# Two-batch windowed attention plus mixture of experts on one core: parts of 16, 12 and 4 tiles, another place for the routing arithmetic, and result rows written by ScalarE

## The chip, the cores and the metric

The kernel runs on 1 core of one Trainium2 chip. The metric is the device time of one execution in microseconds. Five engines work side by side and meet only through semaphores: TensorE (PE; its weight loads are PEld), VectorE (DVE), ScalarE (ACT), GpSimd (POOL) and SyncE (SP, which here only issues DMAs). An engine works through its own list of instructions strictly in the order in which they are written, so that whatever stands behind a wait waits too.

## The reference, cut to what matters

```python
# x: (2, 2048, 128) = 4096 tokens = 32 tiles of 128
x = layernorm(x + attention(x))      # 16 query heads, 4 key/value heads of 8, window of 128 on each side
x = layernorm(x + moe(x))

# moe:
probs   = softmax(x @ router)                      # 8 experts
w, idx  = top_k(probs, 2);  w = softmax(w)
fuse    = silu(x @ gating[e]) * (x @ up[e])        # 128 -> 256, of the two chosen experts
out     = sum over the two of w * (fuse @ down[e]) # 256 -> 128
```

All is float32.

## The kernel before, in words

**Attention steps.** Steps `s` run from -2 to 31, one per tile of 128 tokens, and every engine has its function `step(s)`. A step computes, interleaved, five score items "A" of tile s+2 (only their maxima are wanted) and five items "B" of tile s (exponentials, then the products with the values). Items go in turn through three PSUM banks `pX`. DVE takes the maxima of the A items (`largest_score(a, 0)` to `(a, 4)`, L1311 and L1315), ACT the exponentials of the B items (L1051). PE can't write an item before the one three places earlier is read: item B2 waits for the maximum of A1, item B3 for that of A2. Between these DVE finishes tile s-1: reciprocal `rden` (L1359), `attT` (L1362), residual sum (L1371), statistics (L1378); POOL normalises four tiles at a time (`norm`, L621 to L631).

**Routing.** Eight tiles at a time form a routing group: 21 small DVE operations (`rt_op`, with two exponentials on ACT) give the two experts and their weights. PE counts ranks (`ranks`, L824 and L828), ACT copies them out (L1079), 8 DVE operations (`slot_op`) make the rows' places. `RT_AT`, `RANK_AT` and `SLOT_AT` say in which step each stands. 19 DVE operations per part (`table_op`) make the tables by which the units find their rows and experts. POOL writes each tile's rows, sorted by expert, to DRAM (`sort_rows`, two indirect DMAs per tile, L648).

**Parts and units.** `PARTS` cuts the 32 tiles into parts that are sorted separately: 16, 8 and 8 tiles. A part of n tiles has at most 2n+8 blocks of 128 rows; two blocks are a unit. That makes 20, 12 and 12, together 44 units, numbered k = 0 to 43. In iteration k, PE turns the rows of unit k+1 (`turn_rows`, L940), does gate and up projections of unit k (`gate_up`, L957 to L959), turns the hidden rows of k-1 (L968) and does the down projection of k-2 (L977). ACT rounds rows (L1101), does Silu (L1108), copies turned hidden rows (L1114) and results (`rows_made`, L1120). DVE makes the rest of the rounding (`rest_rows`, L1396) and the product (`hidden`, L1402). SP loads a unit's rows (`rows_in`, L533) and writes its results (L538); before unit 20, the first of part 1, it waits for all sorted rows of that part and for its table.

**The steps left over.** What is left of the steps (32 to 42, among them the whole routing group of the last eight tiles) stands in front of the units' own work in iterations 0, 1 and 3 to 11 (`MOE_STEPS`), on each engine.

**The way back.** POOL gathers both result rows of each tile, two indirect DMAs per tile in the order of the tiles (`rows_back`, L660); before the first tile of a part it waits until every result of that part has been written (`rows_done`). DVE adds them (`combine`, L1414) and normalises, from iteration `COMBINE_AT[t]` on; ACT applies the factors (L1125), SP writes the output (L544).

## Time and profile before

| What | Value |
|---|---|
| Time, median of 3 runs | 593.84 us (588.29 to 595.39) |
| Profiled execution: time, and its span | 593.14 us, 591.3 us |
| PE, PEld | 492.1 us (83%), 301.5 us (51%) |
| DVE | 359.9 us (61%) |
| ACT | 297.9 us (50%) |
| POOL | 241.4 us (41%) |
| Granted TensorE clock, mean | 0.896 |

The span is what the profile sees between the first and the last instruction; 1.84 us of the execution's time lie around it. The shares are averages over very different stretches: attention steps up to about 393 us, then units up to about 558 us, then the last gathers and sums. So the stretches have to be read one by one.

### The profile page before, as it was taken

How to read it: one execution, taken by the hardware profiler on the slowest of the kernel's cores; microseconds unless marked ns; L12 is line 12 of the kernel's file. 1: busy time of each engine (PE TensorE's matmuls, PEld its weight loads, DVE VectorE, ACT ScalarE, POOL GpSimd, SP SyncE). 2: the span in 40 equal slices, each digit the busy share in tenths (PEclk: the TensorE clock that was granted, in tenths of full speed). 3: DMA queues.
4: the chain of work that ended last, by engine and by line, in shares of the span. 5: the costliest groups of instructions: out<-in, count | busy, mean ns of one | idle time of the engine just before them, and what ended most of it. 6: DMA issues, size and time to landing. Idle time of an engine off the chain costs nothing.

```text
span 591.3 us, 12074 instructions
## 1 busy us (share of the span) xinstructions
PE 492.1 (83%) x3864; PEld 301.5 (51%) x3864; DVE 359.9 (61%) x817; ACT 297.9 (50%) x515; POOL 241.4 (41%) x329
## 2 busy tenths in 40 slices
PE   4499899899998999899898987966988999998600
PEld 3263454354453555344453533435877888886500
DVE  0366675576675887667756566553364635767674
ACT  2125554465566656456644544534565555554532
POOL 2131062462533225325435264305714517777072
PEclk9999898798999998899977877788889999999855
DMA  6452324305216352231350012020433535553252
GB/s 159 62 81 56 73 41 105 73 11 135 38 34 147 73 108 56 56 65 54 55 84 18 20 41 86 11 63 25 127 97 96 149 110 135 137 136 96 62 137 58
DMA packets 83948, 46.93 MB, mean 79 GB/s; under 512 B 40496, under 2 KB 79408, under 8 KB 83120
## 3 DMA queue, kind: packets, MB, share of 16 engines
q1 hardware_dynamic: 77184, 36.81, 27.2%
q0 software_dynamic: 4096, 8.40, 5.2%
q10 hardware_dynamic: 2608, 0.95, 0.8%
q8 instruction: 34, 0.56, 0.4%
q14 instruction: 26, 0.21, 0.1%
HBM read 26.47 MB, written 19.40 MB: 78 GB/s over the span
## 4 chain that ended last, share of the span: by engine, by line
PE 61%; DVE 15%; issue 8%; DMA 6%; ACT 3%; SPq 3%; POOL 2%; ACTq 0%; POOLq 0%; DVEq 0%
PE pV L788 13%; DVE mp L1311 6%; PE pX L977 6%; PE pX L713 5%; PE pX L957 4%; PE pX L752 4%; PE pX L959 4%; PE pX L958 3%; DMA xt<-xT 3%; PE pV L968 3%; DVE rden L1359 3%; PE pM L807 3%; PE pX L743 2%; PE pX L764 2%; SPq L427 2%
## 5 line engine op out<-in xcount | busy, mean ns | idle before, releaser
L1311 DVE TENSOR_REDUCE mp<-pX 128x4 f32<-128x1024 f32 (+4 forms) x128 | 150.2, 1186 | 96.6 <-PE pX L717 80.1
L1051 ACT ACTIVATE probs<-pX 128x1024 f32<-128x1024 f32 x152 | 152.8, 1023 | 108.7 <-PE pX L743 94.4
L788 PE MATMUL pV<-probs,vx 128*32 128x512 f32 (+1 forms) x736 | 94.4, 613 | 0.0
L660 POOL DMA_INDIRECT probs<-ys,source x64 | 64.1, 1002 | 48.1 <-issue 31.4
L648 POOL DMA_INDIRECT xs<-xr,slot x64 | 63.0, 984 | 49.5 <-DVE ends L1231 31.4
L752 PE MATMUL pX<-q,kx 50*128 50x512 f32 x248 | 64.5, 518 | 10.1 <-DVE mp L1311 9.4
L713 PE MATMUL pX<-kx,q 48*128 48x512 f32 (+4 forms) x256 | 62.1, 485 | 9.6 <-DMA q<-q_scr 9.6
L1402 DVE TENSOR_TENSOR probs<-probs,pX 128x512 f32<-128x512 f32 x44 | 30.2, 686 | 52.8 <-ACT probs L1108 52.7
L1108 ACT ACTIVATE probs<-pX 128x512 f32<-128x512 f32 x44 | 26.3, 598 | 53.6 <-PE pX L959 53.6
L713 PEld LDWEIGHTS pX<-kx,q 48*128 48x128 f32 x256 | 26.5, 205 | 50.9 <-issue 39.5
L977 PE MATMUL pX<-we,probs 128*128 x352 | 48.4, 282 | 0.7 <-ACT vx L1120 0.7
L957 PE MATMUL pX<-we,qh 128*128 x88 | 40.7, 462 | 8.0 <-issue 4.6
L977 PEld LDWEIGHTS pX<-we,probs 128*128 128x128 f32 x352 | 44.9, 200 | 1.0 <-issue 1.0
L752 PEld LDWEIGHTS pX<-q,kx 50*128 50x128 f32 x248 | 26.4, 210 | 25.0 <-DVE mp L1311 14.8
L959 PE MATMUL pX<-we,ql 128*128 x88 | 36.8, 419 | 0.0
L958 PE MATMUL pX<-we,qh 128*128 x88 | 36.3, 412 | 0.0
L588 POOL CAST kh<-ks 128x512 fp32r<-128x512 f32 x7 | 4.3, 609 | 76.1 <-ACT ks L1028 76.1
L743 PE MATMUL pX<-mask 64*128 64x256 bf16 (+1 forms) x184 | 33.8, 364 | 0.0
L1359 DVE RECIPROCAL rden<-pV 128x128 f32<-128x128 f32 x32 | 30.3, 948 | 5.6 <-PE pV L801 5.6
L601 POOL CAST qh<-qs 128x512 fp32r<-128x512 f32 x7 | 4.3, 609 | 71.4 <-ACT qs L1031 71.4
L788 PEld LDWEIGHTS pV<-probs,vx 128*32 128x32 f32 x736 | 18.3, 116 | 28.6 <-issue 23.2
L968 PE MATMUL pV<-cst,probs 128*128 128x128 f32 x176 | 28.3, 286 | 0.7 <-DVE probs L1402 0.6
(151 smaller groups left out, 827.5 us busy)
## 6 DMA issues: line engine op xcount, KB each, us to landing
q<-q_scr SPq DMA_DIRECT2D x46, 128.0 KB, 4.4
xt<-xs SPq DMA_DIRECT2D x88, 64.0 KB
ys<-vx SPq DMA_DIRECT2D x44, 128.0 KB, 1.9
...
q<-stage SPq DMA_DIRECT2D x128, 2.0 KB
...
```

What stands on the lines that cost most here:

```text
L648: pool.indirect_dma_start(xs[ph][:, :], bass.IndirectOffsetOnAxis(ap=slot[:, t, k:k + 1], axis=0), tile(t), None, bounds_check=ROWS - 1, o ...
L660: pool.indirect_dma_start(yin[:, t % YIN, k, :], None, ys[ph][:, :], bass.IndirectOffsetOnAxis(ap=source[:, t, k:k + 1], axis=0), bounds_c ...
L713: mm = pe.matmul(bank[:, pr, 0:64 * (k1 - k0)], q_cols(t, KA, pr, i, i + 1), k_cols(KA, pr, k0, k1), start=True, stop=True, skip_group_che ...
L752: mm = pe.matmul(bank[:, pr, :], k_cols(KB, pr, k0, k0 + 2), q_cols(t, KB, pr, 0, 4), start=True, stop=True, skip_group_check=True)
L788: mm = pe.matmul(pV[row:row + 32, cols], vx[:, chunk, pr, :], src[:, pr, cols], start=n == 0, stop=True, skip_group_check=True)
L957: pe.matmul(to, xh[:, k % 2, rows], hi, start=True, stop=False, skip_group_check=True)
L958: pe.matmul(to, xh[:, k % 2, rows], lo, start=False, stop=False, skip_group_check=True)
L959: mm = pe.matmul(to, xl[:, k % 2, rows], hi, start=False, stop=True, skip_group_check=True)
L977: mm = pe.matmul(pX[2][:, 1, h * D:(h + 1) * D], hidT[:, k % 2, at:at + P], we[:].bitcast(F32)[:, bass.ds(expert[k, h] + 4 * F + f * D, D) ...
L1051: act.activation(dst, src[:], ACT.Exp).then_inc(exp_done, 1)
L1311: dve.tensor_reduce(mp[:, t % 2, 0, :, i, :], src[:, :, 0:2 * n].rearrange("p r (c v k) -> p r v c k", v=NV, k=32), AX.XY, ALU.max).then_i ...
L1359: dve.reciprocal(rden[:], pV[:, P:2 * P]).then_inc(den_done, 1)
```

## The change

1. `PARTS` becomes 16, 12 and 4 tiles (20, 16 and 8 units, again 44).
2. The routing group of the last eight tiles is still computed as one, but ranked as two groups of 4 tiles (`RANKED`), each with its own ranks, copy and 8 slot operations.
3. In the attention steps DVE's slot, table and first routing operations of a step stand behind the maximum of A0, and the maximum of A1 behind them; before, they stood behind that of A1. Routing groups 0 and 1 are done in three steps and ranked a step earlier. Table 0 moves from steps 28 to 31 into 27, 30 and 31.
4. From iteration 1 on, DVE does its left-over step behind `hidden(k)`, not in front of `rest_rows(k+1)`; ACT does the two exponentials of the last routing group behind `rows_made`. That group is spread over five steps.
5. PE does `gate_up(0)` within step 32, ahead of ranks and output projection.
6. The results' DMAs are issued by ACT, right behind the copy, with a wait for it; SP has none of them.
7. Times at which parts 1 and 2 are sorted, their tables are made and zero rows are written follow the new parts.

The excerpt leaves out what only passes the two rank groups through (`rk` in two buffers, `ranks`, `slot_op`).

```diff
@@ -43,7 +43,7 @@
-PARTS = [(0, 16), (16, 24), (24, 32)]
+PARTS = [(0, 16), (16, 28), (28, 32)]
 NPH = len(PARTS)
 CAP = SEQ + P
 NJ = SEQ // P
@@ -75,9 +75,13 @@
     return next(ph for ph, (a, b) in enumerate(PARTS) if a <= t < b)
+
+RANKED = [(0, 8), (8, 16), (16, 24), (24, 28), (28, 32)]
+
+
 def groups(ph):
-    return PARTS[ph][0] // RT_TILES, PARTS[ph][1] // RT_TILES
+    return [r for r, (a, b) in enumerate(RANKED) if a == PARTS[ph][0]][0], [r for r, (a, b) in enumerate(RANKED) if b == PARTS[ph][1]][0] + 1
@@ -195,20 +199,24 @@
 for m_ in range(NT // RT_TILES):
     s_ = 8 * m_ + 15
     if m_ < NT // RT_TILES - 2:
-        RT_AT.update({s_: (m_, (0, 2), (2, 4), (4, 6)), s_ + 1: (m_, (6, 8), (8, 10), (10, 12)),
-                      s_ + 2: (m_, (12, 14), (14, 16), (16, 18)), s_ + 3: (m_, (18, 18), (18, 20), (20, 21))})
-        RANK_AT[s_ + 3] = m_
-        SLOT_AT[s_ + 4] = m_
+        RT_AT.update({s_: (m_, (0, 2), (2, 4), (4, 6)), s_ + 1: (m_, (6, 11), (11, 12), (12, 13)),
+                      s_ + 2: (m_, (13, 18), (18, 20), (20, 21))})
+        RANK_AT[s_ + 2] = m_
+        SLOT_AT[s_ + 3] = m_
     else:
         last_ = m_ == NT // RT_TILES - 1
-        RT_AT.update({s_: (m_, (0, 2), (2, 5), (5, 9)), s_ + 1: (m_, (9, 12), (12, 15), (15, 18)),
-                      s_ + 2: (m_, (18, 21), (21, 21), (21, 21))} if last_ else
-                     {s_: (m_, (0, 2), (2, 9), (9, 18)), s_ + 1: (m_, (18, 21), (21, 21), (21, 21))})
-        RANK_AT[s_ + 1 + last_] = m_
-        SLOT_AT[s_ + 2 + last_] = m_
+        RT_AT.update({s_: (m_, (0, 2), (2, 2), (2, 2)), s_ + 1: (m_, (2, 7), (7, 7), (7, 7)),
+                      s_ + 2: (m_, (7, 12), (12, 12), (12, 12)), s_ + 3: (m_, (12, 18), (18, 18), (18, 18)),
+                      s_ + 4: (m_, (18, 21), (21, 21), (21, 21))} if last_ else
+                     {s_: (m_, (0, 2), (2, 9), (9, 18)), s_ + 1: (m_, (18, 18), (18, 21), (21, 21))})
+        RANK_AT[s_ + 1 + 3 * last_] = m_
+        SLOT_AT[s_ + 2 + 3 * last_] = m_
+RANK_AT[8 * (NT // RT_TILES) + 12] = len(RANKED) - 1
+SLOT_AT[8 * (NT // RT_TILES) + 13] = len(RANKED) - 1
 EXP_AT = {s_: (e[0], 0) for s_, e in RT_AT.items() if e[1][0] == 0}
-EXP_AT.update({s_: (e[0], 1) for s_, e in RT_AT.items() if any(a_ <= 18 < b_ for a_, b_ in e[1:])})
+EXP_AT.update({s_ - (e[1][0] == 18 and e[0] == NT // RT_TILES - 1): (e[0], 1) for s_, e in RT_AT.items()
+               if any(a_ <= 18 < b_ for a_, b_ in e[1:])})
 def projected(s):
...
@@ -428,13 +436,13 @@
                               q_scr[n % 2][(0, 1, 0)[j], pr].rearrange("p c g t -> p (c g t)")).then_inc(q_in, 16)
         NORMS = 12
-        BEHIND = XIN + 2
-        ZEROS_AT = (10, 20)
-        TABLE_AT = (5, 14)
+        TABLE_0 = {27: (0, 5), 30: (5, 13), 31: (13, TB_OPS)}
+        ZEROS_AT = (19, 26)
+        TABLE_AT = (14, 18)
         COMBINE_AT = []
         for t in range(NT):
             COMBINE_AT.append(max([LAST_UNIT[part_of(t)] + 6] + [n + 1 for n in COMBINE_AT[-1:]]))
-        MOE_STEPS = {k: NT + i for i, k in enumerate((0, 1, 3, 4, 5, 6, 7, 8, 9, 10, 11))}
+        MOE_STEPS = {k: NT + i for i, k in enumerate((0, 1, 3, 4, 5, 6, 7, 8, 9, 10, 11, 12, 13, 14))}
         block = ctx.enter_context(nc.Block())
@@ -502,7 +510,7 @@
                                  ).then_inc(s_z[s // 4 % 2], 16)
                 if s in (15, 17, 19):
                     zeros_last((s - 15) // 2)
-                if s == 28:
+                if s == 27:
                     zeros_behind(0, 0, E)
                 if s == 13:
                     sp.dma_start(we_parts[:, :, 4 * F:].bitcast(F32), wd.rearrange("p (e c) -> p e c", e=E)).then_inc(s_wd, 16)
...
@@ -545,14 +547,10 @@
             for k in range(NU):
                 for ph in range(1, NPH):
-                    e = 2 * (k - ZEROS_AT[ph - 1])
+                    e = 4 * (k - ZEROS_AT[ph - 1])
                     if 0 <= e < E:
-                        zeros_behind(ph, e, e + 2)
+                        zeros_behind(ph, e, e + 4)
                 rows_in(k)
-                if k >= BEHIND:
-                    rows_made(k - BEHIND)
-            for k in range(NU - BEHIND, NU):
-                rows_made(k)
             for b in range(NB):
                 for g in range(4):
                     results_out(b, g)
...
@@ -665,7 +664,7 @@
                 if projected(s) is not None:
                     project(*projected(s))
                 if s == 28:
-                    for t in range(8, 16):
+                    for t in range(12, 16):
                         sort_rows(t)
                 if ln_group(s) is not None:
                     norm(ln_group(s))
@@ -673,6 +672,9 @@
                     split_weights((s - 3) // 2)
                 if 20 <= s < 28:
                     sort_rows(s - 20)
+                if s == 27:
+                    for t in range(8, 12):
+                        sort_rows(t)
             for s in range(FIRST, NT):
                 step(s)
@@ -681,9 +683,9 @@
                     step(MOE_STEPS[k])
                 if 2 <= k < 10:
                     sort_rows(14 + k)
-                if 12 <= k < 16:
-                    sort_rows(2 * k)
-                    sort_rows(2 * k + 1)
+                if 14 <= k < 18:
+                    sort_rows(2 * k - 4)
+                    sort_rows(2 * k - 3)
             for t in range(NT):
                 rows_back(t)
...
@@ -889,6 +892,8 @@
                 if has(s - 1):
                     sums(s - 1)
+                if s == NT:
+                    gate_up(0)
                 if projected(s) is not None:
                     wait(pe, m_evac, SMALL[projected(s)[::-1]] - 1)
                     project(*projected(s))
@@ -985,8 +990,8 @@
                     step(MOE_STEPS[k])
                 if k + 1 < NU:
                     turn_rows(k + 1)
-                gate_up(k)
                 if k:
+                    gate_up(k)
                     turn_hidden(k - 1)
                 if k >= 2:
                     down(k - 2)
@@ -1072,13 +1077,19 @@
                 if m is not None:
                     act.wait_ge(m_psum, SMALL["lg", m])
                     act.copy(lgs[:, 4 * m:4 * m + 4, :], pM[:, 0:4 * E].rearrange("p (t e) -> p t e", e=E)).then_inc(m_evac, 1)
-                m = RANK_AT.get(s)
-                if m is not None:
-                    act.wait_ge(m_psum, SMALL["rk", m])
-                    wait(act, sl_ops, m * SL_OPS)
-                    act.copy(rk[:], pM[:, 0:(RT_TILES + 1) * E].rearrange("p (t e) -> p t e", e=E)).then_inc(m_evac, 1)
+                r = RANK_AT.get(s)
+                if r is not None:
+                    n = RANKED[r][1] - RANKED[r][0] + 1
+                    act.wait_ge(m_psum, SMALL["rk", r])
+                    wait(act, sl_ops, (r - 1) * SL_OPS)
+                    act.copy(rk[:, r % 2, 0:n], pM[:, 0:n * E].rearrange("p (t e) -> p t e", e=E)).then_inc(m_evac, 1)
                 exps(s, 2)
                 exps(s, 3)
+                if s <= NT:
+                    routing_exps(s)
+                exps(s, 4)
+
+            def routing_exps(s):
                 if s in EXP_AT:
                     m, second = EXP_AT[s]
                     if not second:
...
@@ -1118,6 +1128,9 @@
                 if k >= YOUT:
                     act.wait_ge(s_ys[k % YOUT], 16 * (k // YOUT))
                 act.copy(ysb[:, k % YOUT].rearrange("p h d -> p (h d)"), pX[2][:, 1, 0:2 * D]).then_inc(y_done, 1)
+                ph, i = UNIT[k]
+                act.wait_ge(y_done, k + 1)
+                act.dma_start(ys[ph].rearrange("(i h p) d -> i p h d", h=2, p=P)[i], ysb[:, k % YOUT]).then_inc(s_ys[k % YOUT], 16)
             def normalised(t):
                 if t in (a for a, b in SETS):
@@ -1136,6 +1149,8 @@
                     hidden_out(k - 1)
                 if k >= 2:
                     rows_made(k - 2)
+                if k and k in MOE_STEPS:
+                    routing_exps(MOE_STEPS[k])
             hidden_out(NU - 1)
             rows_made(NU - 2)
             rows_made(NU - 1)
...
@@ -1332,14 +1349,12 @@
                 if 0 <= t - 1 < NT:
                     dve.wait_ge(st_done, t)
                     dve.bn_aggr(mv[:, ((t - 1) // 4) % 2, (t - 1) % 4, :], st6[:, (t - 1) % 4, :]).then_inc(mv_done, 1)
-                largest_score(a, 1)
                 if s in SLOT_AT:
                     for n in range(SL_OPS):
                         slot_op(SLOT_AT[s], n)
-                for j in range(4):
-                    if s == 28 + j:
-                        for n in range(5 * j, min(5 * j + 5, TB_OPS)):
-                            table_op(0, n)
+                for n in range(*TABLE_0.get(s, (0, 0))):
+                    if s < 30:
+                        table_op(0, n)
                 g = ln_group(s)
                 if g is not None:
                     y = nw[:, g % 2, 1, :]
@@ -1352,6 +1367,7 @@
                                       ALU.mult, ALU.add).then_inc(ln_seed, 1)
                 for n in range(*ops[0]):
                     rt_op(m, n)
+                largest_score(a, 1)
                 largest_score(a, 2)
                 if 0 <= t < NT:
                     dve.wait_ge(nd_psum, t + 1)
@@ -1364,6 +1380,9 @@
                 largest_score(a, 4)
                 if 0 <= a < NT:
                     negated(a)
+                for n in range(*TABLE_0.get(s, (0, 0))):
+                    if s >= 30:
+                        table_op(0, n)
                 if 0 <= t < NT:
                     if t % 4 == 0:
                         dve.wait_ge(s_z[t // 4 % 2], 16 * (t // 8 + 1))
@@ -1442,11 +1461,13 @@
             rest_rows(0)
             for k in range(NU):
-                if k in MOE_STEPS:
+                if k == 0:
                     step(MOE_STEPS[k])
                 if k + 1 < NU:
                     rest_rows(k + 1)
                 hidden(k)
+                if k and k in MOE_STEPS:
+                    step(MOE_STEPS[k])
                 for ph in range(1, NPH):
                     j = k - TABLE_AT[ph - 1]
                     if 0 <= j < 4:
```

DVE in attention step 27, the step in which routing group 1's slots are made before. (`mp` are maxima of scores, `rt`, `place`, `run`, `slot`, `ends` the slot operations, `rden` the reciprocal.)

```order
L1311 TENSOR_REDUCE mp<-pX 128x2x2
L1334 BN_AGGR mv<-st 128x2
L1311 TENSOR_REDUCE mp<-pX 128x2x2
L1222 TENSOR_TENSOR rt<-rk,run 128x64
L1227 TENSOR_TENSOR rt<-rt,choice 128x64
L1233 TENSOR_REDUCE place<-rt 128x8
...
L1231 CAST ends<-run 128x8
L1311 TENSOR_REDUCE mp<-pX 128x2x2
L1359 RECIPROCAL rden<-pV 128x128
```

The same operations in the change, now in step 26:

```order
L1328 TENSOR_REDUCE mp<-pX 128x2x2
L1351 BN_AGGR mv<-st 128x2
L1239 TENSOR_TENSOR rt<-rk,run 128x64
L1244 TENSOR_TENSOR rt<-rt,choice 128x64
L1250 TENSOR_REDUCE place<-rt 128x8
...
L1248 CAST ends<-run 128x8
L1328 TENSOR_REDUCE mp<-pX 128x2x2 x2
L1375 RECIPROCAL rden<-pV 128x128
```

The eight operations moved from between the second and third maximum to in front of the second; second and third now follow each other.

PE at the passage from the last attention step to the units, before: the sums of tile 31 (`pV<-po,cst`), the ranks (first and last of nine rows), output projection, rows of unit 1, and then the loads of expert numbers and `gate_up(0)`.

```order
L801 MATMUL pV<-po,cst 32x128 x8
L824 MATMUL pM<-msk,mask 128x64
...
L828 MATMUL pM<-msk,mask 128x8
L807 MATMUL pM<-wo_sb,attT 128x128
L940 MATMUL pX<-cst,xt 128x128 x2
L949 TENSOR_LOAD tab
...
L957 MATMUL pX<-we,qh 128x512
```

The change at the same place:

```order
L803 MATMUL pV<-po,cst 32x128 x8
L954 TENSOR_LOAD tab
...
L962 MATMUL pX<-we,qh 128x512
...
L964 MATMUL pX<-we,ql 128x512
L828 MATMUL pM<-msk,mask 128x64
...
L831 MATMUL pM<-msk,mask 128x8
L809 MATMUL pM<-wo_sb,attT 128x128
L945 MATMUL pX<-cst,xt 128x128 x2
```

The six products of `gate_up(0)` stand in front of the ranks and the output projection, which now wait for them.

ACT in one iteration with the first exponential of the last routing group (`rt<-rt`), before:

```order
L1108 ACTIVATE probs<-pX 128x512
L1114 COPY probs<-pV 128x512
L1120 COPY vx<-pX 128x256
L1086 ACT_TABLE_LOAD
L1086 ACTIVATE rt<-rt 128x64
L1101 CAST qh<-pX 128x256
L1108 ACT_TABLE_LOAD
L1108 ACTIVATE probs<-pX 128x512
```

The change:

```order
L1118 ACTIVATE probs<-pX 128x512
L1124 COPY probs<-pV 128x512
L1130 COPY vx<-pX 128x256
L1133 DMA ys<-vx 128x2x128
L1097 ACT_TABLE_LOAD
L1097 ACTIVATE rt<-rt 128x64
L1111 CAST qh<-pX 128x256
L1118 ACT_TABLE_LOAD
L1118 ACTIVATE probs<-pX 128x512
```

The DMA is new on ACT. The exponential stands at the end of iteration 8 instead of the start of it (one unit later), and every iteration has the DMA row.

## Rows read from the trace of the kernel before

**Rows 1.** Busy by stretch: start:end, length, PE, PEld, DVE, ACT, POOL, clock, DMA, GB/s.

```profile
450.00:500.00 50.00, 48.32 (x317) 42.36 (x318) 23.27 (x59) 27.05 (x63) 26.57 (x28) 1.00 0.46 130
```

**Rows 2.** The same view, single attention steps from one reciprocal to the next.

```profile
153.67:163.80 10.13, 9.44 (x92) 4.42 (x92) 7.32 (x12) 6.03 (x10) 2.10 (x1) 1.00 0.35 56
232.84:247.31 14.47, 13.15 (x105) 6.47 (x105) 9.26 (x24) 7.90 (x13) 1.06 (x2) 0.76 0.28 50
329.49:343.10 13.61, 10.89 (x103) 5.31 (x103) 9.27 (x23) 7.33 (x12) 0.25 (x1) 0.85 0.02 7
343.10:356.13 13.03, 10.95 (x88) 5.28 (x88) 8.41 (x17) 6.00 (x8) 9.98 (x11) 0.76 0.17 52
356.13:370.19 14.06, 11.02 (x88) 5.43 (x88) 9.20 (x19) 6.00 (x8) 5.83 (x9) 0.74 0.29 85
```

**Rows 3.** Timeline, DVE and PE, steps 27 to 29: start, us, instruction [idle before].

```profile
339.06 1.23 DVE L1311 TENSOR_REDUCE mp<-pX 128x4 f32<-128x1024 f32 x1 [1.41 <-PE pX L717]
340.21 0.21 DVE L1222 TENSOR_TENSOR rt<-rk,run 128x64 f32<-128x64 f32 x1
...
341.89 0.17 DVE L1231 CAST ends<-run 128x8 int32<-128x8 f32 x1
...
343.24 0.80 PE L752 MATMUL pX<-q,kx 50*128 50x512 f32 x2 [2.11 <-DVE mp L1311]
...
356.27 0.79 PE L752 MATMUL pX<-q,kx 50*128 50x512 f32 x2 [1.57 <-DVE mp L1311]
...
370.33 0.80 PE L752 MATMUL pX<-q,kx 50*128 50x512 f32 x2 [2.61 <-DVE mp L1311]
```

**Rows 4.** Timeline, passage to the units: DVE, PE, POOL.

```profile
392.16 0.42 DVE L1396 TENSOR_TENSOR ql<-pX,qh 128x256 fp32r<-128x256 f32 x1
394.91 0.77 PE L807 MATMUL pM<-wo_sb,attT 128*128 128x128 f32 x2 [2.35 <-DVE attT L1362]
404.58 0.20 POOL L621 TENSOR_TENSOR nw<-nw 128x4 f32<-128x4 f32 x1 [28.57 <-DVE nw L1351]
```

**Rows 5.** Timeline, ACT: Silu of units 7, 12, 19, 20, and a table load.

```profile
430.14 0.60 ACT L1108 ACTIVATE probs<-pX 128x512 f32<-128x512 f32 x1 [1.02 <-PE pX L959]
431.86 1.28 ACT L1086 ACT_TABLE_LOAD   x1
433.15 0.26 ACT L1086 ACTIVATE rt<-rt 128x64 f32<-128x64 f32 x1
452.42 0.60 ACT L1108 ACTIVATE probs<-pX 128x512 f32<-128x512 f32 x1 [2.18 <-PE pX L959]
474.43 0.60 ACT L1108 ACTIVATE probs<-pX 128x512 f32<-128x512 f32 x1 [1.05 <-PE pX L959]
477.36 0.60 ACT L1108 ACTIVATE probs<-pX 128x512 f32<-128x512 f32 x1 [0.96 <-PE pX L959]
```

**Rows 6.** Timeline: first and last sorted row of tiles 24 to 31 (16 DMAs).

```profile
449.38 0.97 POOL L648 DMA_INDIRECT xs<-xr,slot  x1 [17.87 <-DVE ends L1231]
468.53 0.97 POOL L648 DMA_INDIRECT xs<-xr,slot  x1 [0.30 <-issue]
```

**Rows 7.** Timeline: result copies 35 and 43, part 2's 16 gathers, last sum.

```profile
531.42 0.37 ACT L1120 COPY vx<-pX 128x256 f32<-128x256 f32 x1 [0.26 <-PE pX L977]
557.86 0.37 ACT L1120 COPY vx<-pX 128x256 f32<-128x256 f32 x1 [1.44 <-PE pX L977]
561.12 0.99 POOL L660 DMA_INDIRECT probs<-ys,source  x1 [13.62 <-DVE xr L1414]
580.69 1.00 POOL L660 DMA_INDIRECT probs<-ys,source  x1 [0.30 <-issue]
583.28 0.74 DVE L1414 SCALAR_TENSOR_TENSOR xr<-probs,wts,xr 128x128 f32<-128x128 f32 x2 [0.71 <-DMA probs<-ys,source]
```

**Rows 8.** Issue of a DMA by ACT; the results' DMAs by SP, ns min/median/max.

```profile
1.19 0.45 ACTq L1000 DMA_DIRECT2D wo_sb<-wo  x1
...
L538 SPq DMA_DIRECT2D ys<-vx x44: 359/382/1887, 411.5 to 558.3; - x44
```

58 lines of the change are left out of this document (28 added, 30 removed).

## The prediction

> **What bounds the kernel now.** I read the busy time by stretch first. Among the units PE is busy 48.32 of 50 us and ACT 27.05 [rows 1]; Silu of units 19 and 20 lie 2.93 us apart [rows 5], and from unit 12 to 19 it is 22.01 us, 3.14 a unit: units are PE's time. Then the same view cut at DVE's reciprocals gives single attention steps. An undisturbed one takes 10.13 us at clock 1.00, the ones with slot or table operations between two maxima 14.47, 13.61, 13.03 and 14.06 at 0.74 to 0.85 [rows 2]. The timeline says why: DVE idles 1.41 us ahead of the maximum of A1, then does eight slot operations (340.21 to 342.06, 1.85 us) ahead of the maximum of A2, and PE stands 2.11 us until that maximum is taken; two steps with table operations follow, with 1.57 and 2.61 us [rows 3]. Last the end: POOL starts part 2's gathers at 561.12, when the last result (copied at 557.86) has landed, issues 16 at 1.305 us, and DVE's last sum starts at 583.28, 2.59 us after the last issue [rows 7]. So three places can give time: attention steps with routing, the irregular units 7 to 12, the end.
>
> **The change, part by part.**
>
> *Routing ahead of the second maximum.* The three gaps of PE in steps 27 to 29 are 6.29 us [rows 3]. In the change step 26 has the slots ahead of A1's maximum: 1.85 of work in 1.41 of idle time leaves 0.44 us late. Step 27 has five table operations, less work than the slots, and fits; steps 28 and 29 have none. Group 0's slots (14.47 us step, [rows 2]) move likewise. For that step no gap row stands above; I take the 1.85 us less 0.44. Sum: 6.29 - 0.44 + 1.41 = 7.3 us. Above it is the clock: all four steps at 10.13 would save 55.17 - 40.52 = 14.65, less 0.88. Below it are other steps that lose the clock anyway: I take 3 as the lower end, one drop of 4 us more than before (the 14.47 step against 10.13). I take **8**, near the gaps, since the clock also fell in steps with no routing.
>
> *gate_up(0) ahead of ranks and output.* PE idles 2.35 us before the output projection; six products could fill that. But they wait for `rest_rows(0)` (392.16 to 392.58, [rows 4]), which comes later now: six table operations, by eight in 1.85 us [rows 3] 1.4 and somewhat more for two wide ones, stand ahead of step 31's residual sum. I take 1.5 later, so `gate_up(0)` starts near 393.7, and the output projection behind it near 397 where it stood at 394.91. POOL's last `norm` starts at 404.58 on seeds that DVE makes in step 33 [rows 4]; DVE now does that behind `hidden(1)`, and PE's turn of tile 28 (iteration 3) waits for it. Gain and loss cancel: **0**, between -3 and +3.
>
> *Last routing group behind the units' work.* Silu of units 7 and 12 lie 22.28 us apart [rows 5]; five units at 3.03 (mean of 2.93 and 3.14) are 15.15, so routing costs 7.1. It is not free in the change: each exponential still needs two table loads of 1.28 (431.86, [rows 5]), together 2.8 us on ACT in one iteration against its slack of 3.03 - 1.63 = 1.4, so about 1.3 late each; and PE's ranks at the start of iteration 12 wait for five DVE operations that now follow `hidden(11)`, about 1.6, with a second set of ranks 0.5. That is 4.7 to 5.5. I take **+2**, between -1 and +5. The row of the load is followed at once by the exponential (433.15, 0.01 us behind [rows 5]): no drain. The Trainium skill ("ScalarE: Activation LUTs", What ACT_TABLE_LOAD costs) gives a switch about 2.66 us, with 1.38 of drain behind the load; by that the four switches would cost 5.5 us more, and the sum would be 586.5; the trace disagrees.
>
> *ACT issues the results' DMAs.* Price: 0.45 us for an issue on ACT, 0.36 to 1.89 on SP [rows 8], and a wait for its own copy, about 0.1. ACT's busy time per unit goes from 1.63 (27.05 us over 50, times 3.03) to about 2.2 of 3.03. Next on ACT is rounding the rows of unit k+2; it comes 0.6 later and DVE's rest needs another 0.4, with about 1.2 to spare before `gate_up`. SP wrote result 43 soon after its copy already, so nothing is gained: **0**.
>
> *Part 1 is ready later.* It has 12 tiles now, and tiles 24 to 27 need the slots that DVE makes behind `hidden(13)`. From Silu 13: hidden 1.3, slots 1.85, eight DMAs of 1.277 (19.15 over 15, [rows 6]) 10.2, landing 1.4 beyond the last (2.6 from its start, by the gathers of [rows 7]), SP's loads of row numbers and two DMAs about 1.5, landing about 2: 18.3. PE turns unit 20's rows in iteration 19, 1.1 us behind Silu 18, that is at 5 x 3.03 + 1.1 = 16.3. A wait of 2 us, and about 1 for a fall of the clock: **-3**, between 0 and -6. Zero rows (eight at most 1 us each) and table rows are ready earlier. Tiles 28 to 31 are sorted 10.2 us after that, with 16 units to spare.
>
> *The end.* The copy of result 43 was at 557.86 and gathers started 3.26 later. Result 35's was at 531.42, so part 1's 24 gathers start at 534.7; at 1.305 they take 31.3, longer than the eight last units (26.4), so part 2's results are there and its 8 gathers follow without a gap. The 32nd starts at 534.7 + 31 x 1.305 = 575.1, before at 580.69: **+5.6**. DVE, which takes about 1.2 us a tile, has caught up by then. Bounds 4 to 6.
>
> Sum against the profiled execution (593.14, span 591.3): 8 + 0 + 2 + 0 - 3 + 5.6 = 12.6, gives 580.5. The median of the runs is 0.7 above that execution: **581**.
>
> **Rivals.**
>
> 1. *The clock comes back as well.* In the undisturbed step the clock is 1.00 with PE busy 9.44 of 10.13, in the three last ones it is 0.74 to 0.85 with gaps ahead [rows 2, 3]. If gaps are what made it fall, attention gives 13.8 to 15 instead of 8, and the units lose no clock: 574. Against it: other falls have no such gap. The Trainium skill ("TensorE: Matmul & The Clock Gate", Part 1) says that the throttled clock is the default and activity releases it, which speaks for this rival. Chance 0.17.
> 2. *The clock falls elsewhere, and waits among the units are longer.* Attention gives 3, the routing group 0, part 1 costs 5: 3 - 5 + 5.6 = 3.6, that is 590. The order of instructions in which PE waits for ranks, for tile 28 and for unit 20 speaks for it. Chance 0.25.
> 3. *ScalarE becomes the bound* (the other side). If wait and issue take over 1.4 us per unit, ACT exceeds 3.03. At 2.0 (SP's longest issue was 1.89, [rows 8]) every unit gets 0.6 longer; the end hangs on result 35, so 36 x 0.6 = 21.6 against 12.6: 603. It turns the sign where units are 0.35 longer (36 x 0.35 = 12.6), from 1.75 of wait and issue on. Against it stands 0.45 on ACT. Chance 0.06.
> 4. *The smaller last part does nothing*, because POOL must still issue all 64 gathers and the 24 can't start until result 35 is there, late by waits at unit 20: the end gives 0 to 2: 585. Chance 0.07.
>
> **Numbers.** Forecast 0.45 at 581 (575 to 587). Range 572 to 592: it takes in rivals 1, 2 and 4, and leaves out ScalarE as the bound and about 0.1 beyond the edges. About 2% is what can be told from no change: faster means below 582.0. From the forecast 0.26, from rival 1 0.17, from rival 4 0.01: faster 0.44. Slower (above 605.7) only from rival 3 and what I don't see: 0.04. Within: 0.52.
>
> **What would show it.** In attention: no idle time of PE on the maxima in the steps with slots and tables, and steps near 10.2. At the passage: `gate_up(0)` near 393.7 less what attention saved, PE idle ahead of tile 28's turn. Among the units: a DMA row on ACT of 0.45, ACT never late; PE idle at unit 20's rows on a load of SP. At the end: part 1's first gather about 3.3 us behind result copy 35, then 32 gathers without a gap. The forecast is wrong if PE's gaps are gone and steps are still 13 us, if unit 20 waits more than 6 us, or if POOL pauses between parts 1 and 2.

## The result and the profile after

Four runs of the changed kernel gave a median of 573.5 us (566.68 to 578.45), four of the kernel before on the same chip 593.75 (588.29 to 595.39): ratio 0.960 with a 95% interval of 0.9475 to 0.9727, so faster. Two of the four runs of the change, the profiled one among them, are slow ones, over 1.5% above its fastest, and the ratio goes by the other two (571.58 and 566.68). The profiled execution took 575.41 us, its span 573.8, that is 17.5 under the span before. On a second chip (e13, below) the ratio was 0.976 [0.9675, 0.9841]; numbers in square brackets behind a ratio are its 95% interval.

The spans of the two profiled executions fall into three stretches:

| stretch | before | after | gained |
|---|---|---|---|
| start to the reciprocal of tile 31 (end of the attention) | 393.5 | 375.6 | +17.9 |
| from there to the copy of result 35 (last unit of part 1) | 137.9 | 143.5 | -5.6 |
| from there to the end | 59.9 | 54.7 | +5.2 |

The attention first: busy time by stretch of the changed kernel, for the same five steps as [rows 2], the one before the second of them, and one more (190.68, read below) (start:end, length, busy PE, PEld, DVE, ACT, POOL, granted clock, DMA share, GB/s).

```profile
150.48:160.61 10.13, 9.44 (x92) 4.46 (x92) 7.33 (x12) 6.03 (x10) 2.46 (x2) 1.00 0.35 56
190.68:203.80 13.12, 12.58 (x93) 6.06 (x95) 7.62 (x15) 6.09 (x10) 0.00 (x0) 0.74 0.27 42
224.01:237.84 13.83, 12.79 (x107) 6.77 (x109) 9.32 (x23) 6.88 (x12) 7.35 (x18) 0.75 0.14 40
237.84:249.53 11.69, 10.98 (x92) 4.86 (x92) 7.34 (x13) 6.01 (x10) 0.00 (x0) 0.85 0.30 48
323.17:334.85 11.68, 10.66 (x94) 4.82 (x92) 8.40 (x18) 6.45 (x10) 8.94 (x10) 0.85 0.17 53
334.85:344.98 10.13, 8.56 (x88) 4.26 (x88) 7.33 (x13) 6.00 (x9) 6.17 (x7) 1.00 0.35 100
344.98:354.68 9.70, 8.40 (x88) 4.33 (x88) 7.26 (x14) 5.74 (x9) 1.98 (x10) 1.00 0.10 29
```

The quiet step is as long as before. Group 0's slots stand one step sooner than in [rows 2] now, in the step of 13.83 us, and nothing is gained there: from the reciprocal of tile 14 to that of tile 18 it is 45.7 us, 43.0 before. The gain is all behind: from tile 18 to tile 31 it is 126.1 us, 146.2 before. The last three rows take 31.5 us, 40.7 before, and the clock of the last two is 1.00 where it was 0.76 and 0.74. Ahead of them PE's idle time on the maxima changed. Before, PE stood 2.11, 1.57 and 2.61 us for a maximum [rows 3]. These are its longest waits for a maximum in the same part of the change (start, us, instruction, idle before it and its releaser):

```profile
313.95 0.51 PE L766 MATMUL pX<-q,kx 50*128 50x256 f32 x4 [1.01 <-DVE mp L1328]
337.30 0.50 PE L766 MATMUL pX<-q,kx 50*128 50x256 f32 x4 [1.07 <-DVE mp L1328]
347.44 0.50 PE L766 MATMUL pX<-q,kx 50*128 50x256 f32 x4 [1.07 <-DVE mp L1328]
```

The longest of the whole attention is 1.08 us. All of PE's waits for `mp` in the attention sum to 17.4 us before and 10.2 after. The clock is not at 1.00 everywhere: in the step of 190.68 PE is busy for 12.58 of 13.12 us, waits for no maximum, and has 0.74; the longest wait in the step ahead of it is 0.87 us, for POOL. So a low clock without a long wait for a maximum is left too.

The expert stage: timeline rows of PE, then of ACT around a result's DMA, then POOL's gathers around the last result of part 1.

```profile
375.72 0.50 PE L962 MATMUL pX<-we,qh 128*128 x1 [1.96 <-DVE ql L1415]
392.89 0.30 PE L814 MATMUL pM<-cst,xr 128*128 128x128 f32 x1 [3.43 <-POOL xr L629]
429.92 0.18 PE L828 MATMUL pM<-msk,mask 128*128 128x32 bf16 x1 [1.33 <-DVE msk L1216]
464.69 0.50 PE L962 MATMUL pX<-we,qh 128*128 x1 [0.35 <-issue]
```
```profile
464.15 0.37 ACT L1130 COPY vx<-pX 128x256 f32<-128x256 f32 x1 [0.26 <-PE pX L982]
464.56 0.39 ACTq L1133 DMA_DIRECT2D ys<-vx  x1
465.04 0.37 ACT L1111 CAST qh<-pX 128x256 fp32r<-128x256 f32 x1 [0.52 <-ACT vx L1130]
```
```profile
511.46 1.00 POOL L659 DMA_INDIRECT probs<-ys,source  x1 [0.31 <-issue]
522.36 0.99 POOL L659 DMA_INDIRECT probs<-ys,source  x1 [9.90 <-issue]
553.75 1.00 POOL L659 DMA_INDIRECT probs<-ys,source  x1 [0.30 <-issue]
562.93 1.00 POOL L659 DMA_INDIRECT probs<-ys,source  x1 [0.30 <-issue]
```

`gate_up(0)` starts 0.13 us after the reciprocal of tile 31, PE waits 3.43 us at tile 28's turn for the norm, and 1.33 for the mask of the last ranks. Of the 0.35 us at 464.69 the view names no releaser; it calls that "issue". On ACT the rounding of the next rows starts 0.89 us after the copy of a result began, 0.27 before the change. At the end POOL waits 9.90 us, then issues 32 gathers without a pause (522.36 to 562.93; the row of 553.75 is the first of the last part's eight).

### The profile page after: what moved, and what is told of

Same layout as the page of the kernel before. It is cut to its first block, busy times and chain, and to the rows that moved or that the text cites. A ratio compares the mean times of both kernels' runs of the same rounds, so it can differ in the third digit from the quotient of the medians.

```text
span 573.8 us, 12084 instructions
## 1 busy us (share of the span) xinstructions
PE 483.0 (84%) x3865; PEld 296.8 (52%) x3865; DVE 363.3 (63%) x825; ACT 301.1 (52%) x516; POOL 241.3 (42%) x329
## 4 chain that ended last, share of the span: by engine, by line
PE 57%; DVE 17%; issue 10%; DMA 6%; SPq 3%; POOL 3%; ACT 3%; ACTq 0%; POOLq 0%; DVEq 0%
PE pV L790 12%; DVE mp L1328 7%; PE pX L982 6%; PE pX L962 5%; PE pX L715 5%; PE pX L964 4%; PE pX L963 4%; DMA xt<-xT 3%; DVE rden L1375 3%; PE pX L754 3%; PE pV L973 3%; PE pM L809 2%; PE pX L766 2%; PE pX L745 2%; SPq L435 2%
## 5 line engine op out<-in xcount | busy, mean ns | idle before, releaser
L790 PE MATMUL pV<-probs,vx 128*32 128x512 f32 (+1 forms) x736 | 90.7, 591 | 0.0
L754 PE MATMUL pX<-q,kx 50*128 50x512 f32 x248 | 63.0, 505 | 2.5 <-DVE mp L1328 2.0
L982 PEld LDWEIGHTS pX<-we,probs 128*128 128x128 f32 x352 | 43.6, 195 | 1.0 <-issue 1.0
L1415 DVE TENSOR_TENSOR ql<-pX,qh 128x256 fp32r<-128x256 f32 x44 | 18.6, 422 | 26.4 <-ACT qh L1111 25.0
L745 PE MATMUL pX<-mask 64*128 64x256 bf16 (+1 forms) x184 | 31.9, 343 | 0.0
```

The lines of the kernel that those rows point to most:

```text
L754: mm = pe.matmul(bank[:, pr, :], k_cols(KB, pr, k0, k0 + 2), q_cols(t, KB, pr, 0, 4), start=True, stop=True, skip_group_check=True)
L790: mm = pe.matmul(pV[row:row + 32, cols], vx[:, chunk, pr, :], src[:, pr, cols], start=n == 0, stop=True, skip_group_check=True)
L982: mm = pe.matmul(pX[2][:, 1, h * D:(h + 1) * D], hidT[:, k % 2, at:at + P], we[:].bitcast(F32)[:, bass.ds(expert[k, h] + 4 * F + f * D, D) ...
```

## Experiments

Two theories of the attention. **Theory O**: it is the order on DVE. A maximum that is late lets PE stand, and the clock falls for the step behind the gap. **Rival C**: which steps run at the lower clock differs by chance between executions. In the first two groups (e1, e2, e5, e4; e0, e3, e6, e10) single engines stood for 5 to 17 us at a time, so that every kernel, the one before too, took about 100 us longer. A row of e0 on ACT shows what that looks like:

```profile
345.10 0.19 ACT L1079 COPY lgs<-pM 128x32 f32<-128x32 f32 x1 [15.94 <-remote]
```

Those times can't be compared with the others; steps outside such stretches mostly repeat the first profiles' to 0.1 us where the clock is the same (18 of 23 in e0; the others differ by up to 1.0), and only they are read. What mattered was run again in an undisturbed group. "After the attention" below is from tile 31's reciprocal to the end of the span: 197.8 us before, 198.2 after, 200.4 in the second profile of the change. "Tiles 14 to 31" is from the reciprocal of the one to that of the other, and "Silu 0 to 3" from the start of the Silu of unit 0 to that of unit 3.

### e1 and e14: the attention's order alone

Before, with this much of the change (the order inside a step, the routing in three steps, part 0's table in steps 27, 30, 31):

```
-                largest_score(a, 1)
                 if s in SLOT_AT:
...
                 for n in range(*ops[0]):
                     rt_op(m, n)
+                largest_score(a, 1)
                 largest_score(a, 2)
```

> The kernel before with the attention part of the change alone (routing, slots and table operations in front of the maximum of A1; groups 0 and 1 ranked a step earlier; table 0 in steps 27, 30, 31). Theory O (the order of DVE makes PE wait, and the waits make the clock fall): the reciprocals of tiles 14 to 31 lie about 172 us apart as in the changed kernel (189.2 before), the time is 575 to 580 us. Rival C (the clock falls by chance, the order is worth only PE's gaps of about 7 us): about 182 us, and a time of 585 to 588.

> Before, with the change's order in the attention alone. Theory O: the attention's 17 us come in full (tile 14's to tile 31's reciprocal 171.8 us, before 189.2), and since the expert stage is as before, the time is before's less 12 to 18 us, ratio 0.970 to 0.980; the rest to the change (2 to 5 us) is the end's gain less what the units lost. Rival: a shorter attention is eaten by the expert stage of before (POOL's sorting and the last routing are late), so that it gains under 10 us, ratio over 0.983, and the change's other parts are what lets the gain through.

e1: 690.28 us, ratio 0.999 [0.9949, 1.0039], in a disturbed group, so the time says nothing of the expected 575 to 580. One step holds a stretch of some 23 us (35.00 us). The others are the changed kernel's to 0.4 us where the clock is the same, but for the last (8.33 for 7.42). e14, undisturbed: 570.23 us, ratio **0.965** [0.954, 0.9757]; on the same chip the whole change (e13) had 0.976. That is 21 us under the kernel before, more than the 12 to 18 expected. Tiles 14 to 31 took 169.5 us (189.2 before, 171.8 and 173.8 in the change); after the attention 194.9 us. The attention's order alone gives all that the change gives. The rival, that the expert stage of before would eat it, is refuted.

### e2 and e17: one instruction back in its place

The change, with `largest_score(a, 1)` in front of slots, table, norm and routing again:

```
+                largest_score(a, 1)
                 if s in SLOT_AT:
...
-                largest_score(a, 1)
                 largest_score(a, 2)
```

> The changed kernel with one thing undone: the maximum of A1 is again taken ahead of the slot, table and routing operations. Theory O: gaps of 1 to 2 us on PE come back in steps 16 to 18 and 24 to 27, each followed by a half clock, and it is 10 to 14 us slower than the change. Rival C: 3 to 5 us slower, the share of the clock as in the changed kernel (0.92 to 0.93).

> The change with A1's maximum in front of the slot and routing operations again. In the first run of this edit (on a chip with long stretches) the steps of tiles 1 to 24 took 265.5 us to the change's 254.4 on the same kind of chip, and PE's waits for maxima 21 us to 10. Theory M (the place of the maximum carries most of the gain): tile 1's to tile 31's reciprocal 10 to 14 us longer than the change's 309 to 319, ratio to before 0.985 to 0.995. Rival G (the gathering of the routing in fewer steps, and the table's operations in other steps, carry it): under 6 us longer, ratio under 0.985.

e2: 700.07 us, 1.014 [1.0081, 1.0199], disturbed. e17: 591.02 us, ratio **0.999** [0.9945, 1.0037]: the whole gain is gone. Tiles 1 to 31 take 326.96 us (309.57 and 308.70 in the change, 330.82 before), 17 to 18 us longer, where theory M expected 10 to 14. Tiles 14 to 31 take 187.0, and PE's waits for maxima are 16.4 us again, the longest 1.58. Busy time by stretch of e17, its steps of tiles 24 to 28, and PE's waits in them:

```profile
315.53:331.11 15.58, 13.87 (x96) 6.71 (x96) 9.07 (x24) 7.01 (x11) 10.17 (x16) 0.67 0.09 27
331.11:345.20 14.09, 11.18 (x88) 5.06 (x88) 8.43 (x18) 6.00 (x8) 10.74 (x12) 0.76 0.16 50
345.20:357.83 12.63, 10.95 (x88) 5.07 (x88) 7.32 (x12) 5.43 (x8) 4.56 (x5) 0.73 0.25 72
357.83:370.82 12.99, 11.39 (x88) 5.23 (x88) 7.17 (x14) 6.01 (x9) 0.52 (x3) 0.74 0.07 21
```
```profile
333.57 0.80 PE L766 MATMUL pX<-q,kx 50*128 50x256 f32 x4 [1.21 <-DVE mp L1328]
345.33 0.50 PE L754 MATMUL pX<-q,kx 50*128 50x512 f32 x2 [1.58 <-DVE mp L1328]
347.65 0.80 PE L766 MATMUL pX<-q,kx 50*128 50x256 f32 x4 [1.20 <-DVE mp L1328]
```

The steps in which the change had 11.67, 11.68, 10.13 and 9.70 us take 15.58, 14.09, 12.63 and 12.99. The last two have less DVE work than before's and no gap over 1.1 us behind 347.65, yet run at 0.73 and 0.74: here the clock stays low for two steps after the gaps.

### e5: gaps put in

The change, with eight small additions (each waiting for the last) ahead of A2's maximum in steps 4, 6, 8, 10 and 12, which have no routing (left out here: the tile `pad`, its semaphore, and how they are set up):

```
+                if s in (4, 6, 8, 10, 12):
+                    for n in range(8):
+                        dve.wait_ge(s_pad, s_pad_n[0])
+                        dve.tensor_tensor(pad[:, n % 2, :], pad[:, 1 - n % 2, :], pad[:, 1 - n % 2, :], ALU.add).then_inc(s_pad, 1)
+                        s_pad_n[0] += 1
                 largest_score(a, 2)
```

> The changed kernel with eight small DVE additions on a tile of their own between the maxima of A1 and A2 in steps 4, 6, 8, 10 and 12, where nothing stood: the cost of slot operations in that place, by itself. Theory O: PE stands 1 to 2 us in each of them and the clock then falls for 3 to 7 us, so each of the five steps takes 13 to 14 us where undisturbed ones take 10.1, together 15 to 20 us. Rival C: each step is longer by its gap alone, 11.5 to 12, together 7 to 9 us.

723.43 us against 691.2 of before beside it, ratio 1.049 [1.0427, 1.0549]. Busy time by stretch, and two of PE's waits:

```profile
74.37:86.64 12.27, 10.85 (x109) 6.21 (x109) 9.37 (x21) 7.60 (x10) 9.05 (x8) 1.00 0.06 16
86.64:98.55 11.91, 11.43 (x85) 5.36 (x87) 7.67 (x15) 4.89 (x7) 0.00 (x0) 0.72 0.75 163
98.55:113.76 15.21, 9.15 (x94) 4.45 (x94) 12.16 (x20) 7.36 (x10) 10.73 (x20) 0.89 0.16 26
113.76:125.87 12.11, 11.62 (x86) 5.45 (x88) 7.33 (x12) 5.03 (x8) 0.00 (x0) 0.71 0.26 59
```
```profile
86.77 0.80 PE L757 MATMUL pX<-q,kx 50*128 50x512 f32 x2 [0.93 <-DVE mp L1331]
113.90 0.79 PE L757 MATMUL pX<-q,kx 50*128 50x512 f32 x2 [5.41 <-DVE mp L1331]
```

The five padded steps sum to 67.1 us (50.5 in the change's first profile), at clocks of 0.88 to 1.00, and the five behind them, in which nothing was added, to 59.3 (52.7) at clocks of 0.71 to 0.73 instead of 1.00 or 0.86. So gaps made on purpose bring the clock down in the steps behind them: Theory O's second half is shown. The 16.6 us of the padded steps lie in the expected 15 to 20, but they come from waits and additions more than from the clock, which fell one step later than expected. The length of one wait doesn't decide it alone: behind the 0.93 us of 86.77 the step ran at 0.72, while the change's 1.07 us of 337.30 stands in a step at 1.00. The additions were not all of one size: DVE's busy time rises by 1.7 to 2.0 us in three of the steps and by 4.8 in the two in which POOL is busy for 10.7.

### e12 and e13: before and change once more

Both unaltered.

> The kernel before, unaltered, with a profile on a chip of the later groups. The profiles of the changed kernel there hold stretches of 10 to 35 us in which single engines stand for 5 to 17 us and no row names a cause (one step of the attention takes 35 us in place of 11.7, six or so units take 9 to 33 us). Theory of position: before has its own such stretches, also about 100 us, but at other places; outside them its steps are those of the first profile (13 us for the steps of tiles 24 to 27) and its attention some 15 to 18 us longer than the change's, so that the two kernels are equal there only because the stretches weigh more in the change. Rival: before's steps are shorter there than in its first profile (its PE waits hidden), and the gain of the change in the attention isn't there at all.

> The changed kernel unaltered, the measure of this group. On a chip like the first and the third group's: 565 to 578 us, ratio to before 0.955 to 0.975. Tile 1's to tile 31's reciprocal 309 us, with 3 us either way for the steps whose clock differs from one execution to the next.

e12: 586.43 us, 0.994 [0.9854, 1.0022]. Its chip was undisturbed, so its question about the stretches has no answer. But it bears on rival C. Two of its steps, for 14.47 and 13.61 in [rows 2]:

```profile
227.78:242.27 14.49, 13.18 (x105) 6.55 (x105) 9.28 (x24) 7.91 (x13) 1.06 (x2) 0.76 0.29 50
324.30:337.90 13.60, 10.89 (x103) 5.33 (x103) 9.27 (x23) 7.31 (x12) 0.25 (x1) 0.85 0.02 7
```

Tile 14 to 31 took 189.07 us (189.22 in the first profile): on another chip, the same low-clock steps. Over all undisturbed profiles, the nine with the change's order in the attention take 169.5 to 174.4 us for tiles 14 to 31, with no wait for a maximum over 1.08 us; the three with the maximum of A1 in front (before, e12, e17) take 187.0 to 189.2. C fails for this half. It holds for the first half: tiles 1 to 14 take 134.9 to 145.6 us with the one order and 135.7 to 141.6 with the other, and the steps of tiles 3, 5 and 7 took 13.62, 13.17 and 12.31 us in the first execution and 12.18, 10.13 and 10.74 here. These two executions of before give a price, which is an estimate: weighed by the steps' clocks, 72.1 us of tiles 1 to 31 ran at the lower level (1.2 GHz) in the first and 58.4 in the second, and the first is 6.03 us longer, 0.44 us for each. e13: 574.26 us, ratio 0.976 [0.9675, 0.9841]; tiles 1 to 31 308.70 us, as expected. e0, the change in a disturbed group, had 692.24 (1.007 [1.001, 1.0121]).

> The changed kernel itself, unaltered, as the measure for the others of this group. In its first measurement: 573.5 us against 593.75, ratio 0.9601 [0.9475, 0.9727]. Theory O (the order in the attention keeps PE's waits for maxima short, and the clock with them): tile 1's to tile 31's reciprocal 309.6 us or less (before: 330.8 in the profiled execution), ratio 0.95 to 0.97 on a chip like the first. Rival C (the clock differed by chance between two executions): the steps differ from the first measurement's by as much as those of before and change did, some 15 us over the attention. If the whole kernel runs near 690 us, as the last group did, its large stalls of all engines at once are left out and the steps outside them are read.

### e6 and e18: the steps in front of the units' work again

```
-                if k == 0:
+                if k in MOE_STEPS:
                     step(MOE_STEPS[k])
                 if k + 1 < NU:
                     rest_rows(k + 1)
                 hidden(k)
-                if k and k in MOE_STEPS:
-                    step(MOE_STEPS[k])
```
(and ScalarE's `routing_exps` inside the step, as before)

> The change, with VectorE's and ScalarE's remaining steps of the attention and routing in front of the work of a unit again, as before. The prediction took 2 us for this move (-1 to +5). Theory of the prediction: the expert stage is 1 to 4 us longer, most of it in units 7 to 19 (Silu 7 to Silu 19: 46.98 us in the change, 48 to 51 here). Rival N: the units have slack there (only 0.6 us was gained at units 7 to 12), and Silu 7 to 19 stays at 47.0 with 0.5 us either way.

> The change with VectorE's and ScalarE's remaining steps in front of the units' work, as before. The forecast gave the move 2 us (-1 to +5): Silu 7 to Silu 19 would be 48 to 52 us (47.0 in the change), ratio to before 0.965 to 0.98. Rival N: no difference, 47.0 with 0.5 either way.

e6: 686.36 us, 1.000 [0.9943, 1.0064], disturbed just in these units. Its Silu 0 to 3 takes 13.80 us, e0's 16.94. e18: 565.82 us, ratio **0.9615** [0.953, 0.97], its span 562.2. The attention is the change's (308.58 us); Silu 7 to 19 takes 42.98 us, not 48 to 52 and not 47.0, and Silu 0 to 7 28.43 (31.65 in the change). From tile 31's reciprocal to the copy of result 35 it is 136.2 us (143.5 and 143.6 in the two profiles of the change). Both of my expectations missed: the move costs 7.3 us by these profiles. A third one with the change's expert stage, e17's, has 140.8 us there, and against it the move costs 4.5. By the times of whole runs e18 can't be told from the change's 0.960 [0.9475, 0.9727] or 0.976 [0.9675, 0.9841]. The rows of PE's waits of 3.43 and 1.33 us above are gone; the largest on another engine among units 1 to 19 is 1.07.

### e7, e8, e9: three waits taken away one by one

The change itself was not run on the chip of these three, so they are compared with it by stretches of the traces.

e7 (VectorE makes the last norm's seeds ahead of `hidden(0)`):

```
-            def step(s):
+            def step(s, early=False):
...
+                if k == 0:
+                    step(NT + 1, True)
                 hidden(k)
```

> The change, with VectorE's two operations for the last norm ahead of its work for unit 0 (in the change they stand behind two units' work, and PE waits 3.43 us for the norm at the turn of tile 28). Expected by the trace: that wait goes, Silu 0 to Silu 3 takes 14 us in place of 17, and the time is 1 to 3 us under the change. Rival: the wait moves to the next link (the output of the last tiles, or unit 2's rows), and Silu 0 to Silu 5 stays within 1 us of the change's 24.7.

565.89 us, ratio 0.956 [0.9487, 0.9638]. Silu 0 to 3: 13.22 us (16.94 in the change), so the wait's 3.4 us came back, and Silu 0 to 5 (20.98, 24.70 in the change) shows that it did not move on. The attention of its profiled execution had more steps at the lower clock (tiles 1 to 31 318.24 us); it isn't touched by this edit and isn't read.

e8 (ScalarE's DMA of a result one unit later, behind the rounding; `write(k)` is the wait and the DMA that `rows_made(k)` had at its end):

```
                     round_rows(k + 1)
+                if k >= 3:
+                    write(k - 3)
                 silu(k)
```

> The change, with ScalarE's DMA of result k-3 issued behind the rounding of unit k+1's rows, a unit later than in the change. Theory W (the issue in front of the rounding costs the units): the units after the 20th take 2.95 to 3.11 us each in place of 3.21, 4 to 6 us in all. Rival: the units are longer by PE's reads of the expert numbers (e9 shows it, this one does not), and they stay at 3.2. The combination of e7, e8 and e9 had 2.96 for nearly every unit.

576.91 us, 0.9765 [0.9707, 0.9824]. Silu 20 to 34 takes 43.27 us, before's 43.48 and not the change's 45.29: 3.09 a unit, as expected, but 2 us in all and not the expected 4 to 6. Units 12 to 20 are slower instead (26.61 and 3.62 for 25.31 and 2.95), and the whole is not faster than the change. e3 did the same by giving the DMAs back to SP, in a disturbed group:

> The change, with the DMAs of the results issued by SP again, eight units behind. Theory W (ScalarE's issue of about 0.4 us stands ahead of the rounding of the next rows, which comes 0.5 us later, and one unit in two waits for it): Silu 20 to Silu 34 takes 43.5 us in place of 45.3, as before (3.11 a unit for 3.24), unit 43's result copy comes 4 to 6 us sooner, and the whole 3 to 6 us, ratio to the change 0.990 to 0.995. Rival S (the units are slower for another reason: the routing steps behind their work, or the clock): Silu 20 to 34 stays at 45.3 and the time within 1 us. Second rival: the units are faster, but SP's last eight writes go out late and the gathers of the middle part begin no sooner: the units gain, the end does not, time within 1.5 us.

687.07 us, 0.997 [0.9918, 1.0024], e0 beside it 1.007 [1.001, 1.0121]; the ten units from 29 on take 3.12 us on average, in e0 the same ten 3.21. It points the same way, within the intervals.

e9 (PE reads the next unit's expert numbers behind `gate_up(k)`, not ahead of `gate_up(k + 1)`; `experts(k)` is the two reads):

```
                 if k:
                     gate_up(k)
+                if k + 1 < NU:
+                    experts(k + 1)
+                if k:
                     turn_hidden(k - 1)
```

> The change, with PE's reads of the next unit's expert numbers one unit earlier, behind gate_up. If the reads' some 1 us behind the wait for the rows is what holds the units, they take 2.96 each here and 3.2 in e8; if ScalarE's issue holds them, 3.2 here and 3.0 in e8; if each alone gives most of the gain (PE is bound by its own matmuls as soon as either wait is shorter than its slack), both show 2.96 to 3.05. Time: 1 to 9 us under the change.

564.54 us, ratio 0.955 [0.9483, 0.9613], span 559.6. Nearly every unit from 20 on takes 2.96 us, and Silu 0 to 43 143.82 us (157.64 in the change, 151.87 before). PE at a unit in e9: the first product of `gate_up` follows the turned rows at once, without the 0.35 us of idle time of 464.69 above. The change has 19 such gaps ahead of `gate_up`'s first product that its view calls "issue", 9.5 us in sum and up to 1.14; e9 has none.

```profile
452.78 0.38 PE L945 MATMUL pX<-cst,xt 128*128 128x128 f32 x2
452.91 0.48 PE L966 MATMUL pX<-we,qh 128*128 x1
```

ScalarE still issues each DMA ahead of the rounding here. So it was the two together, the reads more than the DMA: rows rounded 0.6 us late, and reads of expert numbers queued on PE behind the wait for them.

### e4 and e15: parts of 16, 8 and 8

Zero rows and tables are made at the iterations of before.

```
-PARTS = [(0, 16), (16, 28), (28, 32)]
+PARTS = [(0, 16), (16, 24), (24, 32)]
...
-RANKED = [(0, 8), (8, 16), (16, 24), (24, 28), (28, 32)]
+RANKED = [(0, 8), (8, 16), (16, 24), (24, 32)]
```

> The changed kernel with parts of 16, 8 and 8 tiles again (the last eight ranked in one group; tables and zero rows at the iterations they had). Theory: the end is 4 to 6 us longer (16 gathers behind the last result in place of a chain of 32 behind result 35), and the second set of ranks and the wait for unit 20 go, which gives back 1 to 2: 3 to 5 us slower than the change. Rival (the end hangs on something else, DVE or the output): same as the change within 1 us.

> The change with parts of 16, 8 and 8 tiles and the last eight ranked in one group. The prediction took 5.6 us (4 to 6) for the smaller last part: then this one is 4 to 6 us slower than the change, and the gathers behind the last unit are 16 in place of 8. Rival: the end is set by POOL's 32 gathers of the second and third part together (they run without a pause from 522.36 us to the end in the change), so that it matters when the second part is ready, which here is sooner: within 2 us of the change.

e4: 694.92 us, 1.008 [1.0039, 1.0118], disturbed. e15: 579.77 us, 0.975 [0.9628, 0.9866], beside e13's 574.26 and 0.976. The medians lie 5.5 us apart, but two of its four runs (575.50 and 573.02) are at e13's time and two (584.04 and 587.01, the profiled one) above it, and the ratios can't be told apart. So this experiment does not decide between the expected 4 to 6 us and the rival's 2. After the attention its profile takes 202.4 us, the change's 198.2 and 200.4. Its rows show where such a gain would come from: POOL waits for result 43 (copied at 551.74) before the last 16 gathers, and from the copy of result 43 to the end it is 33.7 us (33.5 before, 30.0 and 32.1 in the change's profiles).

```profile
539.74 1.00 POOL L657 DMA_INDIRECT probs<-ys,source  x1 [0.30 <-issue]
555.02 1.00 POOL L657 DMA_INDIRECT probs<-ys,source  x1 [14.28 <-DVE xr L1431]
```

In every undisturbed profile with parts of 16, 12 and 4 the end comes 51.2 to 51.6 us after part 1's first gather, whatever the units did (522.36 to 573.8 in the change, 508.22 to 559.6 in e9, 510.69 to 562.2 in e18): POOL's 32 gathers are the bound there, as the first half of e15's rival says. In the disturbed ones it is 71 to 74.

### e10 and e16: the three together

The edits of e7, e8 and e9.

> The change with three edits together: the seeds of the last norm ahead of the first units' work on VectorE (which takes away PE's wait of 3.43 us at the turn of tile 28), the DMA of a result issued by ScalarE one unit later and behind the next rows' rounding, and PE's reads of the next unit's expert numbers behind the unit before. If the three costs are what the trace says: -2 to -3 for the wait, -4 to -6 for Silu 20 onwards (3.24 to 3.11 a unit), -1 to -3 for the reads: 6 to 12 us under the change, ratio to it 0.98 to 0.99. Rival: PE is bound by its own work in most units (a unit's matmuls at full clock take about 3 us), so that each wait taken away only moves to the next one, and the time is within 2 us of the change.

> The change with the edits of e7, e8 and e9 together. e9 alone already has 2.96 us a unit (PE's own matmuls), so e8's part adds nothing to the units: 8 to 12 us under the change from e9, 0 to 3 more from e7 (Silu 0 to 3 in 6.4 + 9.6 us in place of 17), ratio to before 0.935 to 0.955. If the parts added up in full it would be 0.93. If e7's wait only moves on, it is within 1 us of e9.

e10: 675.53 us, 0.988 [0.9761, 0.9998], 16.7 under e0 in its disturbed group, more than the 6 to 12 expected. e16: **554.98 us, ratio 0.942** [0.9336, 0.9497], 19.3 us under the change on the same chip, and faster than both kernels: the best that was run. Silu 0 to 43 takes 137.19 us, after the attention 181.3. After the attention it is 16.9 us under the change, and e9 and e7 (10.4 and 3.7) sum to 14.1. The rest lies at the first units: Silu 0 to 3 takes 9.29 us (16.94 in the change, 13.2 in e7, 16.1 in e9), 3.1 less than the two gains there would leave. e10 has 9.30. Why the two together give more there was not looked into.

## Why the prediction was right or wrong

I forecast 581 us (572 to 592), a gain of 12.6 in the span, and within 2% as the likeliest outcome. It was 573.5, a gain of 17.5 in the span, and faster. That the range held it was partly luck: the sum was wrong in two large terms of opposite sign, the attention (tiles 14 to 31) 9.4 us too low and the expert stage up to result 35 4.6 us too high.

- **Routing ahead of the second maximum: 8 forecast, 17.4 measured** (tile 14 to 31: 189.22 to 171.79). This is the step that failed, by its size. I saw both numbers, the gaps (6.29 us) and the clock (14.65 for four steps), and took the gaps "since the clock also fell in steps with no routing", so that the clock's share stood at almost nothing. Rival 1 is what happened in the attention. That its 574 meets the measured 573.5 is luck: it had the attention at 13.8 to 15 and no loss in the units. By the same weights as in e12, 51.5 us of tiles 14 to 31 ran at the lower level before and 20.7 after; at 0.44 us each that is 13.5 of the 17.4. PE's waits for maxima there fell from 12.7 to 6.1 us. The two sum to more than was gained, so the split is an estimate. e5 shows the link from gap to clock, e17 that one instruction's place decides it. The Trainium skill ("TensorE: Matmul & The Clock Gate", Part 1) has the throttled clock as the default and activity as what lifts it. The traces agree behind long waits (e5, e17: 0.71 to 0.74), but the step of 190.68 has 0.74 with PE idle for 0.54 us. So the clock's part deserved more than 0.17, and what lowers it in such steps stays open: 20.7 us of tiles 14 to 31 still ran at the lower level. Of the four steps I looked at, the last three gave 9.2 us. Around group 0's slots 2.7 us were lost where I counted a gain; in that step before, of 14.47 us, PE has no wait over 0.4 us. Three steps of tiles 22 to 25 that I left out, 12.06, 13.84 and 12.98 us, came to 10.13, 10.54 and 11.67.
- **gate_up(0): 0 forecast, 0 measured, for the reasons given.** Reciprocal 31 to Silu 3 took 22.49 us before and 22.59 after. But the wait at tile 28's turn (3.43 us) was avoidable: without it (e7, e18) the early `gate_up` gives 3.3.
- **Last routing group behind the units' work: +2 forecast, -4.5 to -7.3 measured** by e18 against the three profiles of this expert stage, so the sign was wrong too; 3.3 of it lies at tile 28's turn (Silu 0 to 3, 16.94 to 13.69), which I had put under `gate_up(0)`. I priced what ACT and PE do in the iterations with routing, but not that results of a step which stands behind `hidden(k)` reach PE when it already waits (1.33 us for the mask, 1.1 of issue behind it), nor the clock behind that.
- **ACT issues the results' DMAs: 0 forecast, -1.8 measured** in the 15 units from Silu 19 to 34 (46.42 to 48.24 us). The price of 0.45 was right (0.39). I gave the rounding 1.2 us to spare; PE's reads of the expert numbers stand behind that wait and use it up (e9). Without the DMA ahead of the rounding (e8) units 20 to 34 are 2.0 us shorter, without the reads behind the wait (e9) 3.9.
- **Part 1 is ready later: -3 forecast, -0.6 measured by e15, -1.8 at most.** At unit 20's rows PE waits 1.08 us, for no load. Silu 12 to 20 is 3.3 us longer than before, but e18, with the same parts, has 1.5 of that back, and e15, with the parts of before, has 27.65 us there, 0.6 under the change. So the larger part 1 costs about 0.6 of the 3.3; the rest isn't split further.
- **The end: 5.6 forecast, 5.2 measured** from the copy of result 35 on. The first gather came 3.28 us after it, and 32 followed without a pause, as written. Second profile: 3.1 (the first gather came 5.46 after the copy). The times of whole runs don't confirm it (e15).

Together the expert stage up to result 35 cost 5.6 us, forecast 1; it took back a third of what the attention gave.
